# A wait taken from GpSimd's casts of transposed probabilities in a three-layer attention kernel

## The reference

```python
x = x + 0.5 * _L0_ffn_ref(_layernorm(x, axis=-1), ...)
x = x + _L0_attn_ref(_layernorm(x, axis=-1), L0_attn_w_q, L0_attn_w_kv, L0_attn_w_dense)
x = x + 0.5 * _L0_ffn_ref(_layernorm(x, axis=-1), ...)

# _L0_attn_ref
scores = jnp.einsum('bqgpd,bkgd->bgqpk', q, k) * (SCALE / LAYER_INDEX)
scores = jnp.where(causal[None, None, :, None, :], scores, -jnp.inf)
probs = jax.nn.softmax(scores, axis=-1).astype(x.dtype)
ctx = jnp.einsum('bgqpk,bkgd->bqgpd', probs, v).reshape(b, sq, HEADS * KVC)
return jnp.einsum('bse,eh->bsh', ctx, w_dense)
```

## Time and profile before

| | |
|---|---|
| median of 3 runs | 2666.61 us (2665.38 to 2668.01) |
| the profiled execution's own time | 2667.82 us |
| its span, first to last instruction | 2666.0 us |
| mean granted clock of TensorE | 0.984 |
| busy time: PE, PEld | 2558.9 us (96%), 2367.5 us (89%) |
| busy time: DVE, ACT, POOL | 2126.2 us (80%), 945.0 us (35%), 885.9 us (33%) |

### The profile page before, as it was taken

The page is one execution under the profiler, slowest core; times in us unless marked ns, Lnnn a source line. Parts: engine busy times, 40 slices in busy tenths (PEclk is TensorE's granted clock), DMA queues, the critical chain, the costliest instruction groups (busy, mean ns, idle before and its releaser), DMA issues. The chain is left out here.

```text
span 2666.0 us, 45989 instructions
## 1 busy us (share of the span) xinstructions
PE 2558.9 (96%) x14628; PEld 2367.5 (89%) x14628; DVE 2126.2 (80%) x6046; ACT 945.0 (35%) x2546; POOL 885.9 (33%) x1942
## 2 busy tenths in 40 slices
PE   5999999999996999999999999997899999999998
PEld 4999999999995889898888989896899999999997
DVE  5788888888887788787878787775788888888886
ACT  3111111101113677777777777774211111011100
POOL 3323332333221334343433343333333323332321
PEclk9999999999998999999999999998999999999999
DMA  6000000000011455554544544455100000000000
GB/s 183 23 1 1 1 1 1 1 1 1 1 33 42 81 89 90 88 87 85 90 84 86 90 90 83 87 90 121 56 1 9 9 1 9 9 9 1 9 9 9
DMA packets 378737, 117.30 MB, mean 44 GB/s; under 512 B 338560, under 2 KB 377472, under 8 KB 378496
## 3 DMA queue, kind: packets, MB, share of 16 engines
q1 hardware_dynamic: 378496, 114.36, 22.0%
HBM read 26.24 MB, written 4.19 MB: 11 GB/s over the span
## 5 line engine op out<-in xcount | busy, mean ns | idle before, releaser
L545 PE MATMUL ffn_ring<-ffn_mix_weights,ffn_yT 128*128 128x384 f32 x5760 | 1159.0, 342 | 9.8 <-POOL ffn_mix_weights L1024 7.8
L545 PEld LDWEIGHTS ffn_ring<-ffn_mix_weights,ffn_yT 128*128 128x128 f32 x5760 | 1012.7, 190 | 58.0 <-DVE ffn_mix_sums L711 13.9
L713 DVE SCALAR_TENSOR_TENSOR ffn_mix_sums<-ffn_ring,ffn_w,ffn_mix_sums 128x384 f32<-128x384 f32 x896 | 550.3, 615 | 251.5 <-PE ffn_ring L545 235.6
L1548 POOL CAST attn_probsT<-attn_turned 128x1024 fp32r<-128x1024 f16 (+3 forms) x512 | 348.4, 723 | 524.0 <-DVE attn_probs L1406 513.7
L595 PE MATMUL ffn_ring<-ffn_out_weights,ffn_avT 128*128 128x512 f32 x1536 | 441.9, 399 | 5.3 <-POOL ffn_avT L1014 5.3
L1481 ACT ACTIVATE attn_exponentials<-attn_exponentials,attn_score_neg_max 128x512 f32<-128x512 f32 (+3 forms) x512 | 285.4, 558 | 164.8 <-DVE attn_score_neg_max L1389 164.6
L595 PEld LDWEIGHTS ffn_ring<-ffn_out_weights,ffn_avT 128*128 128x128 f32 x1536 | 283.8, 189 | 33.9 <-POOL ffn_avT L1014 6.6
L1253 PE MATMUL attn_scores<-attn_kT,attn_qT 128*128 128x256 f32 (+2 forms) x1536 | 292.6, 325 | 13.7 <-DVE attn_score_neg_max L1389 10.6
L1253 PEld LDWEIGHTS attn_scores<-attn_kT,attn_qT 128*128 128x128 f32 x1536 | 244.4, 189 | 45.4 <-DVE attn_score_neg_max L1389 13.4
L1253 PE MATMUL attn_ctx<-attn_probsT,attn_v 128*128 128x256 f32 (+2 forms) x1536 | 273.6, 327 | 7.8 <-issue 7.8
L1389 DVE CUSTOM_DVE_ANT_0 attn_exponentials<-attn_scores,causal_row 128x512 f32<-128x512 f32 (+3 forms) x512 | 234.9, 485 | 46.1 <-PE attn_scores L1253 44.9
(11 more groups left out here) (131 smaller groups left out, 2646.6 us busy)
## 6 DMA issues: line engine op xcount, KB each, us to landing
ffn_mix_stage<-in_L_ffn_q_proj_dram SPq DMA_DIRECT2D x32, 128.0 KB, 2.4
ffn_mix_stage<-in_L_ffn_k_proj_dram SPq DMA_DIRECT2D x32, 128.0 KB, 2.5
ffn_mix_stage<-in_L_ffn_v_proj_dram SPq DMA_DIRECT2D x32, 128.0 KB, 2.8
ffn_out_stage<-in_L_ffn_o_proj_dram SPq DMA_DIRECT2D x16, 256.0 KB, 2.9
attn_turned<-attn_probs SPq DMA_TRANSPOSE x256, 4.0
out_dram<-x SPq DMA_DIRECT2D x8, 512.0 KB, 2.9
x<-in_L_attn_x_dram SPq DMA_DIRECT2D x7, 512.0 KB, 8.3
early_stage<-in_L_attn_w_q_dram SPq DMA_DIRECT2D x4, 512.0 KB, 6.1
```

The lines of the kernel that those rows point to most:

```text
L545: last = pe.matmul(bank[:, 0:QKV], yT[:, t % 2, h, k * P:(k + 1) * P], mix_half(e, wh)[:, k], start=(n == 0), stop=(n == 3 * CK - 1))
L713: dve.scalar_tensor_tensor(into, bank[:, 0:QKV], w[:, t, e:e + 1], into, ALU.mult, ALU.add).then_inc(mix_done, 1)
L1548: pool.tensor_copy(cast(i), landed(n, i).rearrange("p (j h q) -> p j h q", h=HL, q=P)).then_inc(t_cast, 1)
```

## The change

GpSimd waits at the start of each slot until VectorE has made the low halves of the probabilities of the next unit (`p_lo`, the count after query tile 0, which is the last of the four). The change takes this wait away. Each cast keeps its own waits: its data has been transposed (`t_landed`), and the context of the unit before is done (`c_ready`).

```diff
             def slot(b, h):
                 u = unit(b, h, 2)
                 if u:
-                    if u[2] + 1 < B * HEADS:
-                        pool.wait_ge(p_lo, done_of(u[2] + 1, 0))
                     for i in reversed(range(QT)):
                         cast_turned(u, i)
                 if 8 <= h < 12 and not (isinstance(b, int) and b >= B - 1):
```

## The result

The changed kernel takes 2803.36 us (median of 4 runs, 2799.1 to 2804.84) against 2667.23 us; the ratio is 1.0509, with a 95% interval of 1.0491 to 1.0527. It is 136 us slower. The profiled execution took 2804.84 us, 137.0 more than the one before. Forecast were 2837 (2720 to 2945): direction and range held, the amount was put 34 us too high.

A forecast was written before the change was run, and what follows sets the result against it. TensorE was taken to set the pace, busy 862.90 of 879.00 us in attention. Delays of 17.0 and 4.5, together 21.5 us per batch item over 7.9 items, gave 170 us: 2666.6 + 170 = 2837 us, range 2720 to 2945.

The forecast's parts named there:

- rival of a gain: Casts and 16-bit splits don't disturb each other; casts end at +2.8 instead of +4.5; 2658 us; chance 0.05.
- three meetings in the trace: Three places where GpSimd work met VectorE instructions with two SBUF inputs: weight split 2.12 us, small cast 1.15 us, power operation 852 ns.
- They take turns, one instruction each: In attention slots, splits and casts alternate, a waiting instruction costing its length less 0.14; 2837 us; chance 0.55.
- GpSimd keeps the port: Upper end: GpSimd runs its four casts, 2.58 us in a row, before VectorE's remaining splits; 2935 us; chance 0.18.
- one-cast-only: Lower end: only the first cast gets in, then VectorE finishes its splits; 59 us more, 2726 us; chance 0.15.
- The holds: Time each held instruction adds: three larger casts 0.90, 0.69, 0.48 us; splits after the first 0.47, 0.34, 0.21 us.
- light slots: Five of the ten slots (heads 0 to 2, 9 to 15), in which TensorE was to be 1.85 us late.
- Room: How late the splits may end before TensorE is delayed: about 1.75 us, or 2.15 with a projection between scores and output product.
- E: End of a slot's last split, counted from the context products' end; forecast 3.59 in ten slots, 2.64 in six.
- The phase settles and each slot pays anew: Next splits start 4.70 us behind the last end, so delay doesn't grow from slot to slot; each slot pays its own.
- S: Start of a slot's splits, counted from the context products' end; forecast to settle at -0.23 us, whatever E is.
- Ten slots: Heads 0 to 2 and 9 to 15, TensorE late by 1.7 us in the mean, 17.0 per item; heads 3 to 8, 4.5.

## Why the prediction was right, and where its sum was off

*The wait was idle time of an engine with much room, and its removal brings an overlap.* Right. The 7.8 us of the earlier trace rows stayed, and the two pairs without contention put the worth of the earlier start at 2.6 and 2.5 us, against the 136 that it cost. The recorded rival of a gain took that row as its bound, and the prediction called it the one wait that could have to do with the casts; it is a wait for the values.

*The split needs what GpSimd reads through.* Shown by three pairs: no reading by GpSimd, no cost; one input in the slow form, no cost; one input in the fast form, cost for exactly those shapes. The three meetings in the trace before had carried the whole argument. The Trainium skill's rule, page "SBUF — State Buffer", section "Who interferes with whom", agrees in what it says of two inputs and of GpSimd reading; whole durations on top of each other, 2899 as an estimate, it did not become, since a waiting instruction ended 0.13 to 0.21 us less than its length behind the other. The 2899 is not what the prediction's own terms give either: with whole casts alone they come to 2883, with whole splits as well to 2930, both as estimates.

*They take turns, one instruction each.* Right, and it had been open for VectorE. GpSimd's casts are issued back to back, and a waiting split gets in after every one, so the upper bound (GpSimd keeps the port) fell. In all of 117 slots read from the trace splits and casts end in turns from the first cast on, for as long as splits are left. VectorE's row of splits doesn't keep it either, and one-cast-only was not the case: run by itself, it gives 2719 us (bound: 2726).

*The holds.* The casts' 0.90, 0.69 and 0.48 were 0.90, 0.70 and 0.47 in the slot above. The splits' 0.47, 0.34 and 0.21 were 0.40, 0.27 and 0.14: a held split saves 0.20 of its length and not 0.14. Four splits take 3.63 instead of the forecast 3.84 in the light slots and 3.29 instead of 3.51 in heads 3 to 8. This 0.2 in every slot is 3.4 us per item and most of the excess (see the sum below).

*Room.* TensorE was forecast to give way from E = 1.75 (2.15 with a projection between). In head 13, E is 3.51 and the slot 1.68 longer: 1.83. In heads 5 and 6 it is 2.46 - 0.61 = 1.85; in head 0, 3.24 - 1.19 = 2.05. The 0.1 between 1.75 and 1.85 could have been read from the rows: in the earlier trace rows the output product starts 0.20 behind the low half of the context, in the changed kernel 0.05 (1389.07 to 1389.12), so there was slack that the 1.75 left out. Heads 2 and 14 have less room than forecast, 2.71 - 1.20 = 1.51 and 3.50 - 1.93 = 1.57 instead of 2.15. In them TensorE waits a second time, at place E, for the low half of the next queries, 0.33 and 0.59 us in each slot:

```profile
PE attn_projections L1266 <- DVE attn_qT L1378: 4.1, 7, 0.6
PE attn_projections L1253 <- DVE attn_qT L1378: 2.6, 8, 0.4
```

The first row is head 14, the second head 2, over the stretch of 1009 us; before, the two came to 1.3 us each. The sum had no term for this wait.

*The phase settles and each slot pays anew.* Right: the splits start 4.70 behind the last end in heads 0, 12 and 13, before as after, and S is -0.13 in head 13 (forecast -0.23). Only in heads 1 and 2 did it settle at -0.58 instead of -0.45, and that is just early enough for the second split to be issued before the cast asks: they behave like heads 3 to 8, E 2.71 instead of 3.4.

*What TensorE would show.* Its waits for the maxima and for the context's low half were forecast at 150 us or more, and its busy time was to stay. Measured are 83.8 us of idle time, 117.0 with the weight loads (107.0 and 10.0), and 51 us more of busy time: part of the delay shows as score products cut in two and as a lower clock. The 384-column split was to take 1.4 us: it takes 1.39 in the slot above, but only 943 ns in the mean, because in heads 1 to 9 no cast gets in ahead of it and it keeps some 610.

*The sum.* Ten slots were put at 17.0 us per item and six at 4.5. Measured: 16.0 and 2.8. In the 16.0 are 1.5 us of lower clock in head 15 and its larger share of the delay, which the forecast had left out, and without the 1.5 the ten would be 14.5. So the splits' and casts' share of the sum was 4.2 us per item too high, of which the holds are 3.4, and the clock, which had no term in it, made good 1.5 of that: so far the closeness is luck. 21.5 against 18.8 us per item, over the 7.9 items assumed, is 21 of the 34 us. Another 10 us are the count: the first and the last item lost 13.5 and 12.5 us only. The 3 us left are the odd slots that the medians leave out (5 us), less what was lost outside these slots.

## What to carry to other kernels

A semaphore wait between two engines without data between them may be there to keep them apart. Before taking it away, list what each side reads: here a GpSimd cast, which reads SBUF, and a VectorE instruction with two SBUF inputs, or with one in the fast form, took turns, and the price fell on VectorE, behind which TensorE waited. The trace of before had the price already, in an odd maximum of some unrelated line (2121 ns against a median of 951): look for instructions whose maximum is far above their median, and see what ran beside them.

An idle engine off the critical path is no reason to start its work earlier. Ask first what the work would then lie beside; here it lay beside PSUM-reading maxima for free.

## What the hardware showed beyond expectation

- A tensor-scalar operation on VectorE from float32 to float16 took 545 ns for 512 columns and 670 for 384. At 256 and 128 columns it was held up by casts (405 to 757 and 342 to 859 ns), at 512 it held up a cast, and at 384 neither.
- An instruction that is held up is not simply shifted by the other's length: a split that waits for a cast ends 0.40, 0.27 or 0.14 us behind it at 384, 256 and 128 columns, where splits that follow one another without casts end 0.53, 0.40 and 0.26 behind the one before. A cast that waits ends 0.90, 0.70 or 0.47 behind the split (1024, 768 and 512 columns); casts in a row end 0.77 and 0.56 behind the one before at 768 and 512.
- A wait of 2.3 us on TensorE in head 15 (2.6 in one case) was followed by a clock of 1.2 GHz in eight of fourteen cases and not in the six others; each fall cost 1.5 us. Why it fell in some items only, these runs don't tell.
